# Feed-forward rows of both layers: on GpSimd, the low part of the weights two items on goes ahead of the weighting of the row's own item

## The reference, cut to what matters

```python
def ffn(x):                                   # x: 1024 tokens x 256
    cw = route(x)                             # 1024 x 16 combine weights, 4 of 16 experts kept
    out = 0
    for e in range(16):                       # gate, up: 128 x 256, down: 256 x 128
        y = silu(x @ gate[e].T) * (x @ up[e].T) @ down[e].T
        out = out + cw[:, e:e+1] * y
    shared = silu(x @ sg.T) * (x @ su.T) @ sd.T
    return out + shared
```

## Time and profile before

| | us |
|---|---|
| median of 3 runs | 868.72 (861.17 to 869.51) |
| the profiled execution, time | 867.31 |
| the profiled execution, span | 865.6 |
| PE busy | 829.0 (96%) |
| DVE busy | 649.7 (75%) |
| ACT busy | 525.2 (61%) |
| POOL busy | 463.4 (54%) |

### The profile page before, as it was taken

One profiled execution on the slowest core, in us unless ns is written; L12 is line 12 of the kernel. 1 busy time (PEld: TensorE's weight loads), 2 busy tenths in 40 slices (PEclk: granted clock), 3 DMA queues, 4 the chain that ended last, 5 costly groups with the idle time before them and its releaser, 6 DMA issues.

```text
span 865.6 us, 14796 instructions
## 1 busy us (share of the span) xinstructions
PE 829.0 (96%) x4544; PEld 626.3 (72%) x4544; DVE 649.7 (75%) x1352; ACT 525.2 (61%) x1106; POOL 463.4 (54%) x397
## 2 busy tenths in 40 slices
PE   8899999999989999989998999999999989999997
PEld 6678788778878888766887888654434447888886
DVE  6898788999998888998386866757788644676553
ACT  4778788778868888763635442335566665454442
POOL 3565555666655556642666766522310526656774
PEclk9999999999999999999999999978999999999999
DMA  5233222322422323212765458311441133334451
GB/s 157 92 98 99 86 97 97 110 95 83 149 74 87 98 96 109 80 50 75 214 217 155 141 166 289 105 57 53 143 148 51 56 98 93 122 124 140 152 161 65
DMA packets 57442, 99.20 MB, mean 115 GB/s; under 512 B 8288, under 2 KB 19040, under 8 KB 57376
## 3 DMA queue, kind: packets, MB, share of 16 engines
q1 hardware_dynamic: 57376, 98.39, 35.5%
HBM read 71.88 MB, written 9.57 MB: 94 GB/s over the span
## 4 chain that ended last, share of the span: by engine, by line
PE 63%; POOL 10%; issue 10%; DVE 9%; ACT 4%; DMA 3%; SPq 0%; POOLq 0%; DVEq 0%; ACTq 0%
PE ps L986 10%; PE ps L972 9%; PE ps L963 9%; PE ps L321 5%; PE ps L387 5%; PE ps L335 4%; POOL q_sin L526 3%; PE ps L1654 3%; PE ps L375 3%; PE ps L348 3%; PE ps L1535 2%; PE ps L362 2%; POOL wqk_lo L520 2%; PE ps L1624 2%; DVE nm L1846 2%
## 5 line engine op out<-in xcount | busy, mean ns | idle before, releaser
L1110 POOL TENSOR_TENSOR ew_lo<-ew_raw,ew_hi 128x768 fp32r<-128x768 f32 x68 | 128.2, 1886 | 56.2 <-ACT ew_hi L1076 48.2
L1062 ACT ACTIVATE hid_hi<-guw 128x512 fp32r<-128x512 f32 x68 | 43.0, 632 | 156.6 <-POOL guw L1126 106.6
L1165 DVE TENSOR_TENSOR hid_lo<-guw,hid_hi 128x512 fp32r<-128x512 f32 x68 | 80.9, 1189 | 72.4 <-ACT hid_hi L1062 72.3
L1126 POOL TENSOR_TENSOR guw<-gu,cwb 128x512 f32<-128x512 f32 x61 | 80.5, 1320 | 91.3 <-issue 73.3
L526 POOL TENSOR_TENSOR q_sin<-q_sw,sin 128x512 f32<-128x512 f32 x62 | 80.7, 1312 | 52.5 <-DMA q_sw<-q_in 51.4
L1846 DVE TENSOR_REDUCE nm<-ps 128x1 f32<-128x512 f32 x128 | 81.6, 684 | 24.3 <-PE ps L1558 23.1
L1741 ACT ACTIVATE e<-ps 128x512 f32<-128x512 f32 x128 | 68.8, 602 | 40.3 <-PE ps L1654 40.1
L986 PE MATMUL ps<-ew_hi,hid_hi 128*128 128x256 f32 x272 | 78.3, 288 | 2.4 <-DVE hid_lo L1165 1.8
L512 DVE SCALAR_TENSOR_TENSOR w<-ex,rden,sgn 128x512 f32<-128x512 f32 (+3 forms) x128 | 79.0, 678 | 0.0
L438 ACT ACTIVATE ex<-sabs,nmax 128x512 f32<-128x512 f32 (+3 forms) x128 | 61.5, 551 | 27.9 <-DVE nmax L486 27.9
L986 PE MATMUL ps<-ew_hi,hid_lo 128*128 128x256 f32 x272 | 76.8, 282 | 0.0
(11 more groups left out here) (190 smaller groups left out, 2404.9 us busy)
## 6 DMA issues: line engine op xcount, KB each, us to landing
ew_raw<-in_ew SPq DMA_DIRECT2D x68, 384.0 KB, 3.3
q_sw<-q_in SPq DMA_DIRECT2D x128, 128.0 KB, 2.0
cwb<-cw_dram SPq DMA_DIRECT2D x61, 256.0 KB, 3.6
wqk_raw<-in_wqk SPq DMA_DIRECT2D x32, 256.0 KB, 2.7
wv_raw<-in_wv SPq DMA_DIRECT2D x32, 128.0 KB, 2.6
wo_raw<-in_wo SPq DMA_DIRECT2D x32, 128.0 KB, 2.2
qs<-stk_q SPq DMA_DIRECT2D x16, 256.0 KB, 3.6
ks<-stk_k SPq DMA_DIRECT2D x16, 256.0 KB, 4.2
```

Source lines behind the costliest of these rows:

```text
L1110: pool.tensor_tensor(ff[f].ew[1][:, i % EW_SLOTS, :], ew_raw[:, i % RAW_SLOTS, :], fp(ff[f].ew[0][:, i % EW_SLOTS, :]), ALU.subtract).then ...
L1126: pool.tensor_tensor(ff[f].guw[:, i % 2, :], ff[f].gu[:, i % 2, :], ff[f].cwb[:, r % CWB_SLOTS, :], ALU.mult).then_inc(sem("guw"), 1)
L1165: dve.tensor_tensor(ff[f].hid[1][:, i % 2, :], ff[f].guw[:, i % 2, :], fp(ff[f].hid[0][:, i % 2, :]), ALU.subtract).then_inc(sem("hid_lo"), 1)
```

## The change

In `row_pool`, POOL's part of a row, `ew_low(i + 2)` stands before `weighted(i)` instead of after it. `row_pool` is called for rows 4 to 33 of layer 0 and 5 to 33 of layer 1; rows 32 and 33 have no `ew_low`, row 17 has no weighting. Nothing else is changed: the same instructions, buffers and semaphores.

```diff
         def row_pool(pool, f, i):
             if (f, i) == (0, ROW_STATS):
                 ln_pool(pool, 2, (0,))
-            weighted(pool, f, i)
             if i + SPLIT_AHEAD < NI:
                 ew_low(pool, f, i + SPLIT_AHEAD)
+            weighted(pool, f, i)
             if (f, i) == (1, T1_AT[1] - 2):
                 ln_pool(pool, 3, (1,))
             if f == 0:
                 a1_row_pool(pool, i)
```

## The result

| | before | after |
|---|---|---|
| median of the runs, us | 869.12 (861.17 to 870.74, 4 runs) | 887.13 (884.22 to 892.4, 4 runs) |
| the profiled execution, us | 867.31 | 884.22 |
| its span, us | 865.6 | 882.5 |

The kernel is slower: the ratio of the times is 1.0231, 95% interval [1.018, 1.0283]. That is clearly more than nothing; whether it is more than 2% the interval leaves open.

A forecast was written before the change was run, and what follows sets the result against it. PE and the POOL, ACT and DVE loop were taken as nearly equal bounds; 14.1 us in layer 1 plus 1.0 in layer 0 on 867.31 gave 882.4, or 883.8 from the median, taken as 883, range 876 to 890.

The forecast's parts named there:

- The loop: POOL and ACT rows: the weighting waits on `ew_low`, `ew_hi`, silu and the previous weighting; 5.07 us per row against 4.38.
- DVE set free: DVE in layer 1 rows: `hid_lo` no longer starts under `ew_lo` and takes about 0.67 us instead of 1.66.
- Rival A: Rows get faster because `hid_lo` is unblocked and gate waits go, PE alone setting rows: 861.7 us, chance 0.04.
- The idle share of PE: PE in layer 1's steady rows: would idle 0.85 us in each 5.07, 17%.
- Rival D: Clock falls as PE idles, with about 3 us before gate 13 of layer 1: 887 if one row falls, chance 0.04.
- Layer 0: Layer 0 rows: gate 20 comes 1.0 us later, at 484.9 instead of 483.92; later rows are hidden behind PE.
- I take nothing: Layer 0 routing rows: DVE's routing operations add no cost, out of a possible nothing to 9 us.
- slips of `hid_lo`: Layer 0: in each of 7 routing rows `hid_lo` slips under the next `ew_lo`, weighting waits 1.28 us: 9 us, chance 0.06.
- from row 20 on PE alone carries the rows: Layer 0 from row 20: PE, busy 83.32 of 84.00 us, hides the longer loop; without cover, up to 9 us.
- queued behind both halves in either order: POOL queue: `rstd`, the rotations of rows 21 to 25 and row 27's bias add follow both halves in either order.
- The sum: Both layers' rows: 14.1 us in layer 1 plus 1.0 in layer 0, 15.1 us, giving 882.4 for the profiled execution.

The follow-up runs named there:

- Experiment 2: Kernel before with the new POOL order in layer 1 only, old order in layer 0: 881.5 us, ratio 1.0138.
- 3: Changed kernel with ACT's silu put ahead of `hid_high` in rows 10 and later: 877.12 us, ratio to the kernel before 1.0072.
- experiment 4: Changed kernel with `ew_high_act(i+2)` first in ACT's row, rows 10 and later: 878.47 us, ratio 1.0105.
- experiments 5 to 8: Kernel before, new order only in layer 0: all but row 18, ratio 1.0075; all but 18, 19, 1.0143; rows 17-19, 1.0001; rows 20-31, 1.0007.

## Why the prediction was right, and where it was not

**The loop, right.** Predicted 5.07 us, measured 5.04 to 5.05, each link within 0.01 us. Experiment 2 shows it alone, 3 shows that it answers to a link one for one, 4 that the rows return to 4.22 without it. Followed row by row (less the 2.55 us by which the execution after came later to gate 5 of layer 1), weighting 9 stands at 752.42 (predicted 752.32), 12 at 770.98 (770.59), 18 at 799.04 (798.47), 33 at 871.46 (871.22): 14.35 us instead of 14.1. The Trainium skill's advice to time GpSimd by the spacing of starts (Perfetto Trace Analysis, GPSIMD Engine Instruction) is borne out: the link is 1.79, not the reported 1.84, as the prediction took it.

**DVE set free, right and worth nothing.** `hid_lo` did fall to 0.69 us, but it lies in no loop that bounds a row. Rival A needed `ew_lo` to be over when `gated` is done; it only starts then (`gated` ends at 844.57 + 0.68 = 845.25, `ew_lo` starts at 845.23). The rule of the Trainium skill on which A drew (SBUF — State Buffer, Who interferes with whom) describes the contention rightly and says nothing on which engine is waited for.

**The idle share of PE, slightly off.** Predicted 0.85 us of idle per row, measured 0.58: PE is busy 4.45 of 5.04 us there. Nothing hangs on it. Rival D's idle stretch before gate 13 came as 2.74 us (estimated 3), with the clock at 1.00 behind it.

**Layer 0, wrong by 5.4 us.** Two steps failed.

The first is the term "I take nothing" for DVE's routing operations. The loop itself ran as forecast up to weighting 9 (439.60 by the before execution's clock, predicted 439.58), but weighting 16 came at 476.83, not 475.57. Three weightings, of items 11, 13 and 15 (at 447.36, 457.94 and 468.93 of the execution after), took 1.74, 1.74 and 1.73 us instead of 1.29, each under the end of DVE's `w_lo`, which has two inputs in SBUF: 3 x 0.45 = 1.3 us, about the whole of the difference. `w_lo` is no routing operation but the low part of weights for layer 1's attention, and the sign of it was there: before the change these three weightings took 1.6 us as well, and the first of the earlier trace rows is one of them. What I bounded (slips of `hid_lo`) was not what came, and it stayed near the low end.

The second is the larger, "from row 20 on PE alone carries the rows". The sum followed the lateness only along `ew_lo` to gate 19 and 20. It had weighting 16 already 3.4 us late, and did not follow that into DVE: `hid_lo` 16, `guw` of item 17, `hid_lo` 17, the adding to x, its statistics, `xn`. The busy share of 83.32 in 84.00 us was read as cover for 14 rows, but the 0.68 us that are missing from it held a wait of 0.32 us for `xn`, and that one place has no cover at all. It cost 2.9 us at gate 21 and, by the clock, 1.5 at gate 22. The statement that `rstd` is "queued behind both halves in either order" was true of the order and no answer to the question, since under the new one POOL waits 1.64 us for `vareps`, DVE's input to it (0.52 before). From row 22 on the step held: gates 22 to 33 took 65.26 us, 65.68 before.

Of the 5.4 us, 1.3 are shown by the durations of the three weightings. The wait for `xn` of about 2.9 is shown by the traces, and experiments 5 to 8 show that neither the order in rows 17 to 19 nor that from row 20 on is enough for it. The 1.5 at gate 22 go with the clock: in all twelve kernels gates 21 to 22 take 7.11 to 7.13 us where it stayed at 1.00, and 7.60 to 8.64 in the five where it did not; no run changed the clock alone.

**The sum.** 15.1 us were forecast on the rows. They lost 20.7, and the two attention stretches of this execution gave 3.8 back. That the profiled execution (884.2) stands so near the forecast for it (882.4) is in part this luck; the medians, 18.0 us apart, are the fairer measure, and 3 us above it.

## What to carry to other kernels

Before two instructions change places on an in-order engine, write down for each what its input waits for, through all the other engines' orders, back to the same engine. If one of them comes round in the new order, the sum of its links from start to start is the new length of the row, and here it could be had to within 0.04 us from the old trace. Then carry the lateness of every output that the change makes late, not only of the one that it makes early, to the next place where the bounding engine already waits for something, however short: a high busy share over many rows does not cover a single place with no slack.

## What the runs showed of the hardware

- DVE's `xn` (TENSOR_SCALAR, one 128x256 input in SBUF and two scalar operands) is held off by POOL as `hid_lo` is. Alone, four of them take 1.38 us; under POOL's instructions 3.89, 5.48 and 5.46. The shortest, median and longest of one are below. The Trainium skill (SBUF — State Buffer, Who interferes with whom) names `tensor_scalar` among the operations that can enter a mode that takes the shared ports. The trace agrees in that `xn` is held off. It shows no faster mode: alone, the starts of `xn` are 0.32 us apart, as those of the statistics over the same 256 columns are (0.33), and `hid_lo`, over twice the columns, takes 0.60. So what makes `xn` wait stays open.

```profile
L242 DVE TENSOR_SCALAR xn<-x,meanvar,rstd x24: 400/407/1943, 6.9 to 756.4; 128x256 f32<-128x256 f32 x24
```

- It works both ways: POOL's weighting of 1.29 us takes 1.74 under DVE's `w_lo` and 1.89 behind DVE's `ew_lo`. Where it lies in the loop, the row grows by as much: weightings 11 and 12 of layer 0 stand 5.51 us apart after the change, 9 and 10 5.09.
- The same idle time does not always bring the clock down. Behind waits of 3.63, 3.19, 3.18 (two kernels), 2.69 and 2.40 us in layer 0, and 1.88 us in layer 1 (experiment 4), it fell; behind 2.74 and 2.69 us before gate 13 of layer 1 (the whole change and experiment 2), and behind 1.90 us (rows 20 to 31 alone) it stayed at 1.00. In the 8 us around the wait of 3.19 PE was busy 4.81; in the 9 us around the wait of 2.74 it was busy 6.33. What tells the cases apart stays open.
